# The mixer's softplus: absolute value and sum with one on ScalarE instead of VectorE

## The reference, cut to what matters

```
zxbcdt = einsum('bld,ed->ble', X, W_in)
z   = zxbcdt[..., :D_INNER]
xBC = zxbcdt[..., D_INNER:D_INNER + CONV_DIM]
dt  = zxbcdt[..., D_INNER + CONV_DIM:]
conv = causal convolution of xBC over time, 4 taps, each channel by itself
xBC = silu(conv + conv_b)
dt  = softplus(dt + dt_bias)
A   = -exp(A_log)
dA  = exp(dt * A)
```

## Time and profile before

| | us |
|---|---|
| median of 3 executions | 1413.08 (1411.3 to 1415.54) |
| the profiled execution, device time | 1406.39 |
| its span in the trace | 1404.7 |
| first and last start of L903, one in each of the 32 steps | 31.5 and 865.8 |

### The profile page before, as it was taken

The page is one execution under the profiler, slowest core; times in us unless marked ns, Lnnn a source line. Parts: engine busy times, 40 slices in busy tenths (PEclk is TensorE's granted clock), DMA queues, the critical chain, the costliest instruction groups (busy, mean ns, idle before and its releaser), DMA issues. The chain is left out here.

```text
span 1404.7 us, 27142 instructions
## 1 busy us (share of the span) xinstructions
PE 1225.8 (87%) x8578; PEld 1070.5 (76%) x8578; DVE 1035.7 (74%) x3118; ACT 866.9 (62%) x1882; POOL 908.1 (65%) x1049
## 2 busy tenths in 40 slices
PE   2899999999999999999999999729998999998960
PEld 2778778778777877877877787519998999998950
DVE  3789989998998999999899899544344344443894
ACT  2677777777777777777777777434444344444453
POOL 0466677667667767766766776516667677663586
PEclk9899999999999999999999999859999999999985
DMA  5600010011001001001100000156766676764565
GB/s 159 198 7 25 26 42 33 24 34 39 24 26 40 31 24 41 32 24 34 39 24 26 34 23 18 44 165 161 183 176 155 169 181 163 168 161 99 188 203 171
DMA packets 112935, 119.90 MB, mean 85 GB/s; under 512 B 19889, under 2 KB 99057, under 8 KB 112881
## 3 DMA queue, kind: packets, MB, share of 16 engines
q1 hardware_dynamic: 97744, 94.58, 21.4%
q0 software_dynamic: 14336, 23.08, 8.7%
q10 hardware_dynamic: 800, 1.57, 0.3%
HBM read 70.63 MB, written 48.56 MB: 85 GB/s over the span
## 5 line engine op out<-in xcount | busy, mean ns | idle before, releaser
L1027 POOL TENSOR_TENSOR mamba_arena<-mamba_arena 128x512 f32<-128x512 f32 (+2 forms) x384 | 383.3, 1009 | 245.0 <-DVE mamba_arena L807 199.4
L456 PE MATMUL bank<-identity,mamba_arena 128*128 128x128 f32 x704 | 112.5, 279 | 53.1 <-DVE mamba_arena L916 27.4
L807 DVE TENSOR_TENSOR mamba_arena<-bank,mamba_arena 128x512 f32<-128x512 f32 (+1 forms) x224 | 136.4, 610 | 15.9 <-PE bank L500 10.0
L456 PEld LDWEIGHTS bank<-identity,mamba_arena 128*128 128x128 f32 x704 | 85.0, 146 | 80.2 <-issue 27.2
L1378 PE MATMUL bank<-xt_hi,wsgu_hi 128*128 128x256 f32 x384 | 114.0, 297 | 17.2 <-DVE xt_lo L1761 13.8
L1378 PE MATMUL bank<-xt_lo,wsgu_hi 128*128 128x256 f32 x384 | 109.6, 285 | 0.0
L1378 PE MATMUL bank<-xt_hi,wsgu_lo 128*128 128x256 f32 x384 | 109.6, 285 | 0.0
L665 ACT ACTIVATE mamba_arena<-bank 128x512 f32<-128x512 f32 x192 | 100.4, 540 | 9.0 <-PE bank L456 6.6
L1378 PEld LDWEIGHTS bank<-xt_hi,wsgu_hi 128*128 128x128 f32 x384 | 74.6, 194 | 18.8 <-DVE xt_lo L1761 14.5
L807 DVE TENSOR_TENSOR mamba_arena<-bank_s,mamba_arena 128x1024 f32<-128x1024 f32 x64 | 77.9, 1217 | 3.5 <-ACT bank_s L705 2.2
L669 ACT ACTIVATE mamba_arena<-x_all,mamba_arena 128x256 f32 (+1 forms) x128 | 69.5, 594 | 12.1 <-DVE mamba_arena L853 7.3
(11 more groups left out here) (368 smaller groups left out, 4479.1 us busy)
## 6 DMA issues: line engine op xcount, KB each, us to landing
experts_arena<-in_egu SPq DMA_DIRECT2D x64, 256.0 KB, 3.7
routed_sum<-zeros SPq DMA_DIRECT2D x1, 8320.0 KB, 27.0
x_all<-in_x SPq DMA_DIRECT2D x32, 256.0 KB, 2.7
token_table<-mamba_arena SPq DMA_DIRECT2D x64, 128.0 KB, 1.7
normed_transposed<-mamba_arena SPq DMA_DIRECT2D x32, 256.0 KB, 2.1
experts_arena<-normed_transposed SPq DMA_DIRECT2D x32, 256.0 KB, 3.8
experts_arena<-in_edown SPq DMA_DIRECT2D x64, 128.0 KB, 3.0
experts_arena<-routed_sum SPq DMA_DIRECT2D x32, 256.0 KB, 3.4
```

The lines of the kernel that those rows point to most:

```text
L456: return nc.tensor.transpose(out, in_, identity[:, :])
L807: return nc.vector.tensor_tensor(out, a, b, op)
L1027: return nc.gpsimd.tensor_tensor(out, a, b, op)
```

## The change

VectorE's two small instructions between the taps go away. ScalarE gets two new ones: |x| by `ACT.Abs` right ahead of its exponential, which now takes -|x| by a scale of -1, and u + 1 by `ACT.Identity` with a bias that points to a column of `ones`, ahead of the logarithm. ScalarE waits for each by semaphore. VectorE's second tap gets a semaphore of its own, `tap0_0`, since nothing else now stands between it and the first.

```diff
                     if real(j0):
-                        eng.wait_ge(dt_nabs, j0 + 1)
-                        nc.scalar.activation(sp["u"], sp["nabs"], ACT.Exp).then_inc(dt_exp, 1)
+                        eng.wait_ge(dt_raw, j0 + 1)
+                        nc.scalar.activation(sp["abs"], sp["x"], ACT.Abs).then_inc(dt_abs, 1)
+                        eng.wait_ge(dt_abs, j0 + 1)
+                        nc.scalar.activation(sp["u"], sp["abs"], ACT.Exp, scale=-1.0).then_inc(dt_exp, 1)
                     if real(j0):
                         eng.wait_ge(projected3, j0 + 1)
                         nc.scalar.activation(half[:, 3], ...)
                     if real(j0):
+                        eng.wait_ge(dt_exp, j0 + 1)
+                        nc.scalar.activation(sp["w"], sp["u"], ACT.Identity, bias=ones[:, 0:1]).then_inc(dt_more, 1)
                         eng.wait_ge(dt_more, j0 + 1)
                         nc.scalar.activation(sp["ln"], sp["w"], ACT.Ln).then_inc(dt_ln, 1)
...
                         nc.vector.scalar_tensor_tensor(half[:, 1], ..., conv_w[:, 1, 0:1],
-                                                       half[:, 1], ALU.mult, ALU.add)
+                                                       half[:, 1], ALU.mult, ALU.add).then_inc(tap0_0, 1)
...
                     if real(j0):
-                        eng.wait_ge(dt_raw, j0 + 1)
-                        nc.vector.scalar_tensor_tensor(sp["nabs"], sp["x"], -1.0, sp["x"], ALU.mult, ALU.min).then_inc(dt_nabs, 1)
-                    if real(j0):
+                        eng.wait_ge(tap0_0, j0 + 1)
                         nc.vector.scalar_tensor_tensor(half[:, 0], ..., conv_w[:, 0, 1:2], half[:, 0], ALU.mult, ALU.add)
                         nc.vector.scalar_tensor_tensor(half[:, 1], ..., conv_w[:, 1, 1:2], half[:, 1], ALU.mult, ALU.add).then_inc(tap1_0, 1)
-                    if real(j0):
-                        eng.wait_ge(dt_exp, j0 + 1)
-                        nc.vector.tensor_scalar(sp["w"], sp["u"], 1.0, None, ALU.add).then_inc(dt_more, 1)
```

More of the change, by code:

```diff
@@ L172, in build @@
         shift_x, shift_2 = view(NB), view(NB)
-        sp = {k: view(NB, NH) for k in ("x", "nabs", "u", "w", "d", "ln", "num", "den", "q", "inv", "sp", "dt", "a", "a_grid")}
+        sp = {k: view(NB, NH) for k in ("x", "abs", "u", "w", "d", "ln", "num", "den", "q", "inv", "sp", "dt", "a", "a_grid")}
         logit = view(NB, NE + 1)
@@ L304, in build @@
         dt_raw = sem("dt_raw")
-        dt_nabs = sem("dt_nabs")
+        dt_abs = sem("dt_abs")
         dt_exp = sem("dt_exp")
@@ L325, in build @@
         newest0, newest2 = sem("newest0"), sem("newest2")
+        tap0_0 = sem("tap0_0")
         tap1_0, tap1_1, tap0_2, tap1_2 = sem("tap1_0"), sem("tap1_1"), sem("tap0_2"), sem("tap1_2")
```

## The result

The changed kernel takes **1408.01 us** (median of 20 executions, 1396.24 to 1419.19), the kernel before, on the same chip, 1412.53 (20 executions, 1407.53 to 1417.52): the ratio is **0.9965**, 95% interval 0.9948 to 0.9982. It is faster by 4.5 us where about 21 were forecast, and 1408 lies outside the predicted range of 1378 to 1405.

The account below looks back on a forecast made before the run. A step was taken as bound by VectorE's row through the taps, then TensorE's row. 31 steps x 0.675 = 20.9 us off the profiled 1406.39 gives 1385.5; plus 6.7 for the median, 1392 us, range 1378 to 1405.

Parts of the forecast that it names:

- The ports: VectorE's small SBUF instructions wait for the GpSimd operation they meet; L903 takes 0.82 us against 0.18 with GpSimd idle.
- The four taps in a row: VectorE's taps start 0.39, 0.51 and 0.39 us apart; the last ends 1.19 us earlier and TensorE's 0.88 us wait goes.
- ScalarE: Its two new instructions cost nothing, covered by VectorE's four taps; w takes between 0.22 and 0.35 us.
- The prediction's estimate from the Trainium skill: By the page's rule, w on ScalarE costs 0.12 us more a step than it frees, some 4 us: 1417.
- d meets GpSimd's third operation: In VectorE's softplus chain, d starts at 515.84, ends 0.03 us behind that operation at 516.33, 1.46 us earlier.
- q or sp: Which VectorE chain instruction xw catches: q gains 0.58 us, sp 0.96; q in three steps of four, 0.675 a step.
- rival 1: q passes xw in every step of VectorE's chain: 31 x 0.96 = 29.8 us gained, 1383; chance 0.17.
- TensorE, the step that failed: TensorE's second wait, at L571, grows from 0.38 to 0.77 us; of 1.26 us waiting about 0.6 to 0.7 stay.
- Rival 4: d itself is caught by xw; TensorE's first wait goes and comes back whole at L571: 1413; chance 0.07.
- The margin of the median: The kernel before's median lies 6.7 us above its profiled execution; this was added to 1385.5, giving 1392 us.

Follow-up runs that it names:

- e2: The changed kernel with u + 1 back on VectorE between the second and third tap, only the absolute value staying on ScalarE: 1404.61 us.
- e5: The kernel before with only GpSimd's product xw moved to its idle time ahead of y_sum0: 1393.97 us.
- e4: The changed kernel with GpSimd's xw for sequence 1 moved from behind the halo copies to an earlier idle slot, ScalarE's decays waiting for a later signal: 1365.23 us.
- e3: The kernel before with only u + 1 moved to ScalarE, the absolute value still on VectorE: 1406.66 us.
- e1_fill: The changed kernel with five unread products on TensorE filling its wait ahead of the running sums: 1384.36 us.
- e8: e4 with a 900-element VectorE memset behind the taps, ahead of d: 1382.68 and 1386.07 us in two executions, 1411.47 and 1412.52 in two others.

## Why the prediction was wrong, point by point

- **The ports.** Right. VectorE's small SBUF instructions end with GpSimd's; e2 to e5 confirm it (d from 0.76 us to 0.16 in e5, sp from 0.74 to 0.18 in e4, num stretched to 0.84 in e3, and u + 1, back on VectorE, at 0.16 in e2, where it had been 0.55). So the two engines hold each other up without a semaphore too, other than the opening says of engines in general.
- **The four taps in a row.** Right: 0.39, 0.50, 0.40 apart against 0.39, 0.51, 0.40, and TensorE's first wait is gone.
- **ScalarE.** Right: w took 0.29 us, between the bounds of 0.22 and 0.35, and was ready 0.47 us ahead of d. The prediction's estimate from the Trainium skill ("ScalarE: Activation LUTs", section "Rules for kernel authors") would have made it a loss of 4 us; the 0.29 us cost nothing, since ScalarE's row isn't the one waited for.
- **d meets GpSimd's third operation.** Right: 0.49 us forecast and measured.
- **q or sp.** Mis-sized. The prediction gave q three chances in four of being caught, from two starts 0.02 us apart. In 30 of 32 steps sp was caught, for a gain of 0.92 us an undisturbed step instead of 0.675. That is rival 1, which had a chance of 0.17. The chain kept its time, q 0.44 us behind the end of GpSimd's third operation in both working and trace; xw came 0.48 behind it instead of 0.42, since its first copy started 0.03 later and took 0.02 longer. That is 0.06 us, close to what such rows can tell, and it decided who was caught. Had only this term been off, the time would have been 1383, as rival 1 has it; e1_fill, with no half-clock stretch in the mixer, takes 1384.36.
- **TensorE, the step that failed.** The prediction said: "Its second wait does not go", "a wait of 0.77 instead of 0.38", and then took the sum as if a wait that moves costs what it lasts. The wait did grow, to 0.56 us where the step is undisturbed; the working's 0.77 went with q caught. What the prediction didn't do is ask what the clock makes of it: it moved TensorE's idle time from a place behind wide projections, where 0.87 us had let the clock stay at 1.00, to a place between products of 64, 48 and 16 columns, where 0.56 us goes with a fall to 0.50 fifteen times in 32 steps. So the cost of the moved wait, which the sum put at nothing beyond its length, took 17.3 of 26.1 us in the profiled execution (by e1_fill; 19.6 of 28.5 by the undisturbed steps). No row of before shows such a stretch in the mixer, but the granted clock is in the page, and a term for it, with "none" as one bound, belonged in the range.
- **The rivals.** None had this mechanism. Rival 4, which also ended near the result (1413), is refuted: d is not caught by xw.
- **The margin of the median.** The prediction put the profiled execution's distance to the median (6.7 us) on top. The profiles' times after the mixer lie 9 us apart, and before's is the shortest of all; adding the distance was right.

Left open: what exactly the chip weighs, and so why 0.56 us of waiting gives 15 stretches in the profile of after and 1 in that of another kernel with the same wait (e8); what lowered the clock in e8's two long executions; and why the part behind the mixer lies between 533.6 and 542.9 us.

## What to carry to other kernels

When a change shortens one engine's row, see where TensorE's waiting goes, not only how much is left, and read the granted clock of the changed stretch: with a wait of 0.56 us between thin products, each step whose clock fell lost another 1.1 to 1.5 us here. Filling the wait with idle products was worth 24 us of 1408 (e1), and making it vanish, with 0.50 us off the step, 43 (e4). A small SBUF instruction of VectorE beside a busy GpSimd costs what is left of the GpSimd operation that it meets, so the price of removing one is found by asking who meets that operation next; moving the GpSimd operation into a slot where GpSimd waits was worth more here (18 us in e5, 43 in e4) than the change itself (4.5). If the executions of a kernel scatter more than those of the kernel before it, look at the clock of each one before trusting a median or a single profile.

## What the runs showed of the hardware

- TensorE's granted clock fell to 0.50 again and again on an engine that was busy 263.7 of 270 us, with waits of 0.56 us (after), and stayed at 1.00 on one with waits of 0.87 us elsewhere in the step (before, e5) or with none (e4).
- The drops came once a step for nine steps, 27.3 us apart, from 484 to 702 us, after 236 us without any. Executions of one program differ: e8 took 1382.68 us at a clock of 0.960 and 1412.52 at 0.933.
- A VectorE instruction that GpSimd stretches ends between two GpSimd operations that stand back to back: L903 ended at 515.08, 0.03 us after the second, with the third still running to 516.30. GpSimd doesn't show it: its second and third operation take 2.42 us together in before (513.88 to 516.30), with L903 and L911 stretched beside them, and 2.42 in after (451.84 to 454.26), with d alone.
- VectorE's taps, which read the bank and one operand in SBUF, take 0.47 or 0.48 us in every step shown, also beside a GpSimd operation.
